# An attention stage's running-maximum chain is spread over more steps, and its sums are made a step later

## The reference

```python
q, k, v = x @ Wq + bq, x @ Wk + bk, x @ Wv + bv          # per head
alpha = ((q[dst] * (k[src] + e)).sum(-1)) / sqrt(d)       # e = edge_attr * We
m     = segment_max(alpha, dst)
ex    = exp(alpha - m[dst])
denom = segment_sum(ex, dst)
agg   = segment_sum((ex / denom[dst])[:, :, None] * (v[src] + e), dst)
out   = layernorm((agg + skip) @ Wo + bo + x)
```

## Time and profile before

| what | value |
|---|---|
| time, median of 3 runs | 6076.83 us (6073.62 to 6087.9) |
| the profiled execution, its time | 6069.62 us |
| the profiled execution, its span | 6067.6 us |
| busy share of the span | PE 64%, DVE 60%, ACT 47%, POOL 71% |
| mean granted TensorE clock | 0.776 |
| the attention stage in the trace | about 163 to 1431 us |

### The profile page before, as it was taken

How to read it: one execution, slowest core, us unless ns; L and a number is a source line. 1 busy time by engine, 2 the same in 40 slices (tenths; PEclk the granted TensorE clock), 3 DMA queues, 4 the chain that set the end, 5 groups by cost and what they waited for, 6 DMA issues and landing times. The chain is left out here.

```text
span 6067.6 us, 93535 instructions
## 1 busy us (share of the span) xinstructions
PE 3856.3 (64%) x20652; PEld 3144.4 (52%) x20652; DVE 3649.1 (60%) x11761; ACT 2834.3 (47%) x6936; POOL 4297.3 (71%) x4477
## 2 busy tenths in 40 slices
PE   5567767765666767678888876344343446666665
PEld 4566666664555555546556554333333346665443
DVE  6788888886988888667777774111001034445665
ACT  3788888882111111355555563111111158884444
POOL 2677777663777777767777776677777777777775
PEclk8787787787999898878888887555555579898777
DMA  4444444453655555622223324332222245553223
GB/s 125 123 134 129 128 129 128 123 117 103 189 148 147 147 148 148 126 64 74 74 74 74 74 74 62 100 77 77 77 75 75 73 115 168 163 164 89 59 59 46
DMA packets 485366, 649.31 MB, mean 107 GB/s; under 512 B 120187, under 2 KB 332938, under 8 KB 484822
## 3 DMA queue, kind: packets, MB, share of 16 engines
q0 software_dynamic: 155552, 345.75, 22.9%
q1 hardware_dynamic: 329271, 297.58, 18.2%
HBM read 495.44 MB, written 150.71 MB: 106 GB/s over the span
## 5 line engine op out<-in xcount | busy, mean ns | idle before, releaser
L694 POOL DMA_INDIRECT kv_ring<-keys_values,gather_i x880 | 860.8, 978 | 363.9 <-issue 247.9
L2105 POOL DMA_INDIRECT rows_by_src<-arena,key x880 | 869.3, 988 | 309.7 <-issue 260.2
L694 POOL DMA_INDIRECT e_ring<-filter_rows,gather_i x880 | 838.8, 953 | 304.8 <-issue 268.0
L694 POOL DMA_INDIRECT e_ring<-table,gather_i x880 | 845.7, 961 | 287.2 <-issue 264.6
L694 POOL DMA_INDIRECT arena<-table,gather_i x880 | 850.6, 967 | 278.8 <-issue 266.7
L2089 PE MATMUL rs_ph<-nodes,arena 128*128 x1664 | 424.4, 436 | 667.7 <-ACT arena L2098 615.6
L2089 PEld LDWEIGHTS rs_ph<-nodes,arena 128*128 128x128 f32 x1664 | 365.5, 324 | 726.9 <-issue 726.9
L2081 DVE TENSOR_SCALAR arena<-arena,part 128x512 f32<-128x512 bf16 x220 | 113.6, 519 | 949.2 <-PE rs_ph L2089 898.3
L1565 PE MATMUL e_pa<-e_msg,e_hot 128*128 128x128 f32 x3520 | 552.5, 308 | 37.0 <-DVE e_msg L1768 30.2
L743 DVE TENSOR_TENSOR arena<-arena,e_pa 128x128 f32 x1760 | 496.9, 282 | 110.8 <-PE e_pa L1565 81.9
L2331 PE MATMUL gl_sum_f<-arena,gl_hot_f 128*128 128x128 f32 x1760 | 292.8, 318 | 425.3 <-DMA arena<-table,gather_i 198.5
(11 more groups left out here) (461 smaller groups left out, 9821.1 us busy)
## 6 DMA issues: line engine op xcount, KB each, us to landing
rows_by_src<-e_filler SPq DMA_DIRECT2D x256, 260.0 KB
arena<-rows_by_src SPq DMA_DIRECT2D x256, 260.0 KB
at_rows<-local_rows SPq DMA_DIRECT2D x220, 128.0 KB
e_rows<-local_rows SPq DMA_DIRECT2D x220, 128.0 KB
arena<-local_rows SPq DMA_DIRECT2D x220, 128.0 KB, 3.3
e_attr<-edge_attr SPq DMA_DIRECT2D x880, 25.0 KB
kv_ring<-keys_values,gather_i POOLq DMA_INDIRECT x880
e_ring<-table,gather_i POOLq DMA_INDIRECT x880
```

Of the source, the lines that this page charges most:

```text
L694: pool.indirect_dma_start(ring[:, r, u, :], None, table, bass.IndirectOffsetOnAxis(index, 0)).then_inc(arrived[r], 16)
L2105: pool.indirect_dma_start(self.table, bass.IndirectOffsetOnAxis(place, 0), self.out[:, r, u, :], None, bounds_check=SLOTS_R - 1, oob_is_er ...
```

## The change

LAG goes from 8 to 9, so `exps`, `weigh` and `message` work on batch s-9. `edge_hot` and `total` work on s-10 and the additions on s-11. The node parts start two steps later (`NODE_AT`). The chain of a chunk runs now over five steps: `score` and `turn_scores` in phase 1, `scan_runs` and `turn_runs` in phase 2, `walk` and `turn_carries` in phase 3, `carries`, `scan_all` and `return_max` in phase 0 of the next four steps, `shift` and `exponents` in its phase 1. In PE's step the totals stand before the turns. In DVE's step `products` come first, and the last addition comes before `message`. The outer product of `rank_one` is put beside the first two sums in `pa`, whose four sums are laid out as two banks of 512. The inverse roots are made a step later, and before the exponents. SP's block is not edited.

```diff
-LAG = 8
+LAG = 9
-NODE_AT = [BUCKET_ENDS[n] + LAG + 1 for n in range(NB)]
+NODE_AT = [BUCKET_ENDS[n] + LAG + 2 for n in range(NB)]
-        pq, pa = pb("pq", [P, 2, U, 256]), pb("pa", [P, U, 256])
+        pq, pa = pb("pq", [P, 2, U, 256]), pb("pa", [P, 2, 512])
+        sum_of = lambda u: pa[:, u // 2, u % 2 * C_END:(u % 2 + 1) * C_END]
+        outer = pa[:, 0, 2 * C_END:3 * C_END]
             def turn_scores(n):
-                at_least(pe, rescaled, n, None)
+                at_least(pe, shifted, n, None)
+                at_least(pe, fallen, 3 * n, None)
             def rank_one(n):
-                pe.matmul(p_row[:, R_ACC], lhs, fac[0:1, :], start=True, stop=False)
-                pe.matmul(p_row[:, R_ACC], lhs, minus[0:1, :], start=False, stop=True).then_inc(ranked, 1)
+                at_least(pe, added, U * (n * CB - 1) + 2, None)
+                pe.matmul(outer, lhs, fac[0:1, :], start=True, stop=False)
+                pe.matmul(outer, lhs, minus[0:1, :], start=False, stop=True).then_inc(ranked, 1)
# PE's loop
                 node_sums(s)
+                km = s - LAG - 1
+                if 0 <= km < BATCHES:
+                    if km % CB == 0:
+                        rank_one(km // CB)
+                    total(km)
                 if ph == 1 and 0 <= n < CHUNKS:
                     turn_scores(n)
                 if ph == 2 and 0 <= n < CHUNKS:
                     turn_runs(n)
+                if ph == 3 and 0 <= n < CHUNKS:
                     turn_carries(n)
-                if ph == 3 and 0 <= n < CHUNKS:
-                    return_max(n)
                 if ph == 0 and 0 <= n - 1 < CHUNKS:
-                    rank_one(n - 1)
-                if 0 <= s - LAG < BATCHES:
-                    total(s - LAG)
+                    return_max(n - 1)
# ACT's loop
-                if 0 <= s - LAG < BATCHES:
-                    edge_hot(s - LAG)
+                if 0 <= s - LAG - 1 < BATCHES:
+                    edge_hot(s - LAG - 1)
+                if ph == 0 and 0 <= n - 1 < CHUNKS:
+                    carries(n - 1)
                 if s + 1 < BATCHES:
                     turned_hot(s + 1)
+                for lag, w in ((FIRST, 0), (SECOND, 1)):
+                    if node_due(s, lag + 1) is not None:
+                        inverse_root(node_due(s, lag + 1), w)
+                if ph == 1 and 0 <= n - 1 < CHUNKS:
+                    exponents(n - 1)
                 if 0 <= s - 1 < BATCHES:
                     keep_values(s - 1)
                 if 0 <= s - LAG < BATCHES:
                     exps(s - LAG)
                 if ph == 1 and 0 <= n < CHUNKS:
                     spreads(n)
-                if ph == 2 and 0 <= n < CHUNKS:
-                    carries(n)
-                if ph == 3 and 0 <= n < CHUNKS:
-                    exponents(n)
                 take_nodes(s)
# DVE
             def rescale(n, which):
                 dve.wait_ge(ranked, n + 1)
+                dve.wait_ge(summed, 2 * n * CB + 1)
# DVE's loop
-                ka, km = s - LAG - 1, s - LAG
+                ka, km = s - LAG - 2, s - LAG
-                if chain and ph == 2:
-                    scan_runs(n)
-                if chain and ph == 3:
-                    scan_all(n)
                 if 0 <= s - 1 < BATCHES:
                     products(s - 1)
+                if ph == 1 and 0 <= n - 1 < CHUNKS:
+                    shift(n - 1)
+                if ph == 2 and 0 <= n < CHUNKS:
+                    scan_runs(n)
+                if ph == 3 and 0 <= n < CHUNKS:
+                    walk(n)
                 if adding and ka % CB == 0:
                     rescale(ka // CB, which[0])
                 if adding:
                     add(ka, 0, which[0])
                 if 0 <= s - 2 < BATCHES:
                     head_sums(s - 2)
                 if adding:
                     add(ka, 1, which[1])
-                if chain and ph == 1:
+                if ph == 0 and 0 <= n - 1 < CHUNKS:
+                    scan_all(n - 1)
+                if ph == 1 and 0 <= n < CHUNKS:
                     score(n)
-                if chain and ph == 2:
-                    walk(n)
-                if chain and ph == 3:
-                    shift(n)
+                if adding:
+                    add(ka, 2, which[2])
                 if 0 <= km < BATCHES:
                     weigh(km)
                 if adding:
-                    add(ka, 2, which[2])
+                    add(ka, 3, which[3])
                 if 0 <= km < BATCHES:
                     message(km)
-                if adding:
-                    add(ka, 3, which[3])
```

More of the change, by code:

```diff
@@ L804, in stage_attention @@
         low, fall, fac, minus = sb("low", [1, H]), sb("fall", [1, H]), sb("fac", [1, C_END]), sb("minus", [1, C_END])
-        pq, pa = pb("pq", [P, 2, U, 256]), pb("pa", [P, U, 256])
+        pq, pa = pb("pq", [P, 2, U, 256]), pb("pa", [P, 2, 512])
+        sum_of = lambda u: pa[:, u // 2, u % 2 * C_END:(u % 2 + 1) * C_END]
+        outer = pa[:, 0, 2 * C_END:3 * C_END]
         p_turn = p_row = pb("p_turn", [P, 512])
         T_IN, T_OUT, T_CARRY = slice(0, P), slice(0, P), C_END
-        R_ACC, R_LAST, R_FIRST = slice(0, C_END), slice(C_END + 2, C_END + 2 + P), slice(C_END + 2 + P, C_END + 2 + 2 * P)
+        R_LAST, R_FIRST = slice(C_END + 2, C_END + 2 + P), slice(C_END + 2 + P, C_END + 2 + 2 * P)
         pn = pb("pn", [P, 4, P])
@@ L929, in total @@
                         at_least(pe, added, U * (k - 1) + u + 2, None)
-                    ins = pe.matmul(pa[:, u, 0:C_END], hot[:, q, u, :], msg[:, q, u, :], start=True, stop=True)
+                    ins = pe.matmul(sum_of(u), hot[:, q, u, :], msg[:, q, u, :], start=True, stop=True)
                     if u % 2:
@@ L1070, in take_nodes @@
                     act.activation(of_bucket(c.query, at, 0, F), pn[:, 3, :], ACT.Copy).then_inc(taken, 1)
-                for lag, w in ((FIRST, 0), (SECOND, 1)):
-                    if node_due(s, lag) is not None:
-                        inverse_root(node_due(s, lag), w)
             for s in range(SLOTS_N):
@@ L1205, in rescale @@
                 dve.wait_ge(ranked, n + 1)
+                dve.wait_ge(summed, 2 * n * CB + 1)
                 at_least(dve, added, n * CT, None)
                 to = acc[:, bass.ds(which, 1), :].rearrange("p one f -> p (one f)")
-                dve.scalar_tensor_tensor(out=to, in0=p_row[:, R_ACC], scalar=1.0, in1=to, op0=ALU.add, op1=ALU.mult).then_inc(rescaled, 1)
+                dve.scalar_tensor_tensor(out=to, in0=outer, scalar=1.0, in1=to, op0=ALU.add, op1=ALU.mult).then_inc(rescaled, 1)
             def add(k, u, which):
@@ L1216, in add @@
                 to = acc[:, bass.ds(which, 1), :].rearrange("p one f -> p (one f)")
-                dve.tensor_tensor(to, to, pa[:, u, 0:C_END], ALU.add).then_inc(added, 1)
+                dve.tensor_tensor(to, to, sum_of(u), ALU.add).then_inc(added, 1)
             def join_heads(n):
@@ L1259, in _ @@
                 ph, n = phase(s)
-                chain = 0 <= n < CHUNKS
-                ka, km = s - LAG - 1, s - LAG
+                ka, km = s - LAG - 2, s - LAG
                 adding = 0 <= ka < BATCHES
                 which = loaded_values(nc, c.bucket_d, ka, DVE_ENGINE, NT - 1) if adding else None
-                if chain and ph == 2:
-                    scan_runs(n)
-                if chain and ph == 3:
-                    scan_all(n)
                 if 0 <= s - 1 < BATCHES:
                     products(s - 1)
+                if ph == 1 and 0 <= n - 1 < CHUNKS:
[4 more added lines that the diff above has]
+                    walk(n)
                 if adding and ka % CB == 0:
```

## The result

The changed kernel takes 6362.31 us (median of 4 runs, 6353.60 to 6365.79), the kernel before 6079.64 beside it: a ratio of 1.0459 [1.0446, 1.0472], 283 us slower. The forecast was 6320 us in a range of 6190 to 6400. The profiled execution took 6364.40 us, with a span of 6362.7.

What follows compares the result with a forecast made beforehand. No engine was full; DVE's 20.5 us was the best for a 22.2 us chunk. Late rows close a loop of 4.6, 6.3 and 15.5, taken as 26.8 us; 53 loops add 244 us, giving 6320 us, range 6190 to 6400.

Steps and rivals of the forecast that it cites:

- SP's queue holds the rows: SP waits at the run-break load for scan_all, so rows of batch 4n+1 behind it land 4.6 us after the scan.
- ACT stands 4 to 5 us in every chunk: ACT waits for late rows before turned_hot: scan_all moves 6.8 us, a margin of 2.4 us becomes minus 4.4.
- The loop takes 26.8 us: Once per chunk through SP, ACT and DVE: parts sum to 26.4 us, taken as 26.8 with hand-overs, against 22.2 before.
- Term 1: SP's queue and DMA: from the end of scan_all to rows landed, 1.3 + 3.3 = 4.6 us.
- Term 2: ACT from the landed rows to the end of the exponents, 6.3 us.
- Term 3: DVE from weigh to the end of the next scan_all, 20.5 - 5.0 = 15.5 us.
- What is late next: the exponents: In ACT's order the exponents stand behind the late rows; DVE's weigh waits for them, about 6 us in every chunk.
- the second rival: Loop closes through ACT alone: floor of 24.3 us a chunk, 111 us more, time 6188 us; chance 0.12.
- The chain's waits on PE shrink: DVE's waits for PE results, mostly in the running-maximum chain, 1.7 us a chunk, shrink with the chain spread out.
- The opposite rival: SP's lateness stays hidden and DVE loses its waits on PE: 60 us gained, time 6017 us; chance 0.08.

## Why the prediction was right, and where it was not

- *SP's queue holds the rows.* Right. Rows landed 4.6 us after scan_all in the mean over the chunks, as predicted; moving the one load takes the whole loss away, and the late wait alone in the kernel before brings 243 us of it.
- *ACT stands 4 to 5 us in every chunk.* In every chunk, yes; the size was 7.2. The working set the move of the scan against a margin between two times of the old schedule, and made the move too short: from the old scan's end at 720.41 to the next products at 725.35, then 1.7 to the end of the second addition and 0.96 for the two scans, it is 7.6 us, not 6.8, and ACT would stand 5.2. The rest goes with ACT's new order, in which it has no work of its own between its carry and the rows: in the mean over 36 chunks 2.8 us pass from the carry's start to the scan's end and 4.6 to the rows; less 0.2 for the carry itself, that is the 7.2.
- *The loop takes 26.8 us.* It takes 27.7. The trace splits it, in means over the 35 whole loops between 300 and 1300 us. Term 1 is 4.6 us, as worked out. Term 2, to the end of the exponential, is 6.3, as worked out (its 0.3 for the exponential stands in no line of the earlier trace rows; the trace before has 0.304 us at L1039). From there to weigh are 0.3. Term 3, from weigh to the end of the next scan_all, is 16.5 where 15.5 was used: DVE is busy in it for 14.3 us and idle for 2.2, among them 0.75 of issue ahead of products, 0.4 of additions behind additions and 0.4 behind PE. So the sum is short by 1.0 in DVE's part; of the 0.4 added for the hand-overs 0.3 was needed. The total went from 244 to 283 us, within the range.
- *What is late next: the exponents.* This step failed in part. DVE's standing for ACT is 5.7 us a chunk where "about 6" was predicted, but 2.5 of them are at the inverse roots. Making the exponents earlier gained nothing, and the kernel before, which has no exponents there, closes nearly as long a loop through ACT's copies and the totals. The prediction followed one path around the loop and called it the loop; the runs show three of almost one length, through the exponents, the roots and the totals. With exponents, roots and turns moved ahead, ACT's own round remains, so the second rival was no other outcome but the floor under the forecast.
- *The chain's waits on PE shrink.* Right, 1.7 to 0.5 us a chunk.
- *The opposite rival: with no late rows the change gains 60 us.* What decides is what the prediction said, the lateness of the rows, but the price was too high: 11 us without further edits. The new order had put two additions side by side (19.2 us), and DVE's waits on PE only halved. With that mended the gain is 0.45%, with the early register loads 0.6%. A third buffer for the run breaks, which would take the wait away at its root, wasn't tried.

## What to carry to other kernels

When a step is moved, list all that waits for its semaphores, the loads in the DMA queues first, and then all that is issued behind those loads in program order: here an unedited line of SP's, harmless before thanks to a margin of 2.4 us, cost 283. A load that waits late belongs behind the loads with nearer deadlines; check the margin of each load, not only whether it waits today. And before naming the place where a loop closes, look for the other crossings between the same two engines: a stall that leaves one can appear at the next.

## What the runs showed of the hardware

The granted clock of PE fell where PE stood. Windows of 2 us in the changed kernel, through one late row load (the column behind POOL's is the clock):

```profile
324.00:326.00 2.00, 1.27 (x10) 1.02 (x10) 1.94 (x8) 0.00 (x0) 1.42 (x2) 1.00 0.28 74
326.00:328.00 2.00, 0.32 (x3) 0.03 (x1) 1.41 (x6) 0.00 (x0) 0.60 (x1) 1.00 0.79 202
328.00:330.00 2.00, 0.00 (x0) 0.00 (x0) 1.81 (x7) 1.55 (x3) 0.00 (x0) 0.50 0.57 160
330.00:332.00 2.00, 1.96 (x8) 1.86 (x8) 0.00 (x0) 1.97 (x7) 0.84 (x1) 0.50 0.39 122
```

PE is busy 0.32 us and then not at all; the clock goes from 1.00 (2.4 GHz) to 0.50 (1.2 GHz) and is still there when PE works again. Over 300 to 1300 us the clock is 0.72 against 0.82, and 0.82 again with the break load last. PE's busy time in a chunk rises from 695 x 22.2 / 1000 = 15.4 us to 654 x 27.7 / 1000 = 18.1 for the same matmuls, 90 a chunk in both. A stall thus made the work behind it longer, which the sum had no term for. Little of it shows in the loop: term 2 came out as worked out, and in term 3 DVE stood 0.4 us behind PE.

Two additions side by side, the second of which waits for the first by a semaphore, leave DVE idle 0.21 us (91 times, 19.2 us); with an unrelated instruction of 0.20 us between them the idle time is gone.
